# A fused attention kernel: rows of q and k loaded by groups of two pairs, two chunks of values computed after the first scores, no dummy products before them

## What is computed

```
x = x + attn_a(ln(x))    # causal softmax attention, 16 heads of 8, with a position bias
x = x + ffn(ln(x))       # gate r = sigmoid(xr W_r), k = relu(xk W_k)^2, r * (k W_v)
x = x + attn_b(ln(x))    # linear attention: q, k = elu(rope(.)) + 1, kv = sum k v
x = x + ffn(ln(x))

# attn_a, per head h:
attn = q k^T / sqrt(8) + slope[h] * min(key - query, 0)
out  = softmax(attn where key <= query) v ;  out @ W_O.T
```

## Time and profile before

| What | us |
|---|---|
| Median of 3 runs | 347.98 |
| The profiled execution, its own time | 344.1 |
| Its span, first to last instruction | 341.8 |
| Busy: PE, ACT, DVE, POOL | 308.0, 287.1, 164.1, 56.2 |

### The profile page before, as it was taken

The page is one execution under the profiler, slowest core; times in us unless marked ns, Lnnn a source line. Parts: engine busy times, 40 slices in busy tenths (PEclk is TensorE's granted clock), DMA queues, the critical chain, the costliest instruction groups (busy, mean ns, idle before and its releaser), DMA issues.

```text
span 341.8 us, 6101 instructions
## 1 busy us (share of the span) xinstructions
PE 308.0 (90%) x2332; PEld 134.1 (39%) x2332; DVE 164.1 (48%) x426; ACT 287.1 (84%) x409; POOL 56.2 (16%) x56
## 2 busy tenths in 40 slices
PE   3895999999999999999999999999999956889795
PEld 2562232333333223223333223233222836778574
DVE  6851143266634041614340331334530987978785
ACT  7546899998989999999899999989999565882962
POOL 5895000400000000101000100000000161900630
PEclk9997899999999999999999999999999999999999
DMA  7455565850012000000000000000000000000013
GB/s 227 125 148 172 177 189 178 247 163 19 0 44 80 3 0 2 0 2 0 2 4 0 2 0 2 0 2 0 2 1 2 0 3 0 0 2 0 2 32 92
DMA packets 13264, 16.43 MB, mean 48 GB/s; under 512 B 1488, under 2 KB 8016, under 8 KB 13136
## 3 DMA queue, kind: packets, MB, share of 16 engines
q1 hardware_dynamic: 13232, 16.01, 15.5%
HBM read 6.56 MB, written 2.62 MB: 27 GB/s over the span
## 4 chain that ended last, share of the span: by engine, by line
ACT 36%; PE 35%; issue 12%; DVE 7%; SPq 4%; DMA 4%; POOL 1%; ACTq 0%; DVEq 0%
ACT probs L511 23%; PE ps L1062 14%; PE ps L1041 10%; ACT parts_last L511 5%; PE ps L895 5%; ACT x L511 4%; PE ps L890 2%; DMA kr<-parts_mid 2%; PE ps L1119 2%; ACT scr L520 2%; SPq L344 2%; DMA kc<-in_krows 1%; DVE scr L839 1%; SPq L333 1%; POOL rstd L419 1%
## 5 line engine op out<-in xcount | busy, mean ns | idle before, releaser
L511 ACT ACTIVATE probs<-ps 128x1024 f32<-128x1024 f32 (+5 forms) x223 | 169.4, 857 | 13.7 <-PE ps L1041 12.7
L1041 PE MATMUL ps<-qr,kr 64*128 64x512 f32 (+6 forms) x592 | 109.9, 424 | 9.4 <-ACT probs L511 5.2
L1041 PEld LDWEIGHTS ps<-qr,kr 64*128 64x128 f32 x592 | 49.8, 185 | 126.4 <-ACT probs L511 84.5
L1062 PE MATMUL ps<-probs,vaug 128*9 128x512 f32 (+5 forms) x892 | 98.3, 498 | 0.4 <-DVE probs L783 0.4
L783 DVE TENSOR_TENSOR probs<-probs,cs 128x512 f32<-128x512 f32 x60 | 41.2, 689 | 100.1 <-ACT probs L511 100.0
L419 POOL TENSOR_TENSOR rstd<-veps,neghalf 128x4 f32<-128x4 f32 x16 | 16.6, 1036 | 232.7 <-DVE veps L597 232.7
L511 ACT ACTIVATE parts_last<-ps 128x1024 f32<-128x1024 f32 (+9 forms) x49 | 44.9, 971 | 1.4 <-PE ps L1041 1.2
L895 PE MATMUL ps<-w,scr 128*128 128x128 f32 x288 | 35.3, 278 | 3.2 <-ACT scr L470 2.7
L895 PEld LDWEIGHTS ps<-w,scr 128*128 128x128 f32 x288 | 33.5, 192 | 7.0 <-ACT scr L470 3.6
L1062 PE MATMUL ps<-parts_last,vaug 128*9 128x512 f32 (+9 forms) x196 | 25.4, 549 | 0.0
L1062 PEld LDWEIGHTS ps<-probs,vaug 128*9 128x9 f32 x892 | 13.6, 88 | 28.1 <-issue 17.2
(11 more groups left out here) (107 smaller groups left out, 239.0 us busy)
## 6 DMA issues: line engine op xcount, KB each, us to landing
x<-in_x SPq DMA_DIRECT2D x8, 256.0 KB, 4.2
qr<-parts_mid SPq DMA_DIRECT2D x16, 128.0 KB, 3.1
kr<-parts_mid SPq DMA_DIRECT2D x16, 128.0 KB, 3.0
kr<-att SPq DMA_DIRECT2D x8, 128.0 KB, 3.1
qr<-att SPq DMA_DIRECT2D x8, 128.0 KB, 3.2
qr<-parts_last SPq DMA_DIRECT2D x8, 128.0 KB, 3.6
kr<-parts_last SPq DMA_DIRECT2D x8, 128.0 KB, 3.2
out_y<-x SPq DMA_DIRECT2D x4, 256.0 KB, 2.3
```

The costliest lines, as they stand in the source:

```text
L511: nc.scalar.activation(slot[:, 2 * u:2 * u + 2, w0:w1], ps[:, b:b + 2, w0:w1], ACT.Exp).then_inc(exp_done, 1)
L1041: ins = nc.tensor.matmul(ps[:, 2 * (n % 3) + v, w0:w1], kr[kb // TPC][a:a + SIDE, j, P * (kb % TPC):P * (kb % TPC + 1)], qr[unit.c][a:a + ...
L1062: ins = nc.tensor.matmul(ps[32 * v:32 * v + V1, 6 + unit.lane, w0:w1], vaug[:, kb, V1 * h:V1 * (h + 1)], probs_slot(unit)[:, v, w0:w1], st ...
```

## The change

- The product rows are copied by groups of two pairs. A DMA of the same kind carries half the bytes, and there are 16 for each (chunk, q or k), where there were 8. Before the `branched` wait SP issues group 1 of `FIRST` (12 DMAs); behind it groups 2, 3 and 0 of `FIRST` (36 DMAs), then 16 each for the other five tensors. The waits on rows go by group. The heads are permuted in the weights and the mask to suit.
- k of chunk 1 is computed ahead of the turn of chunk 2, and its high part is taken ahead of the copy of that turn. `values(1)` goes to bank 3 and is taken by DVE.
- The values of chunks 2 and 3 are computed behind the branch: chunk 2's between the scores of unit 0 and unit 1, chunk 3's behind unit 1's, both through bank 7 and copied by DVE.
- `branched` no longer waits for all parts, and all 8 dummies of this stretch are gone.
- The slots that the exponentials of units 0, 2 and 3 go to are permuted; ACT waits before unit 3 for the last values.

```diff
-            def product_rows(n, m, side):
+            def product_rows(n, m, g):
...
-                            sp.dma_start(dst[n][PROD_ROW + r:P:STRIDE, PAIRS // 2 * side:PAIRS // 2 * (side + 1), :].bitcast(F32),
-                                         parts[n][m][i][SIDE * side:SIDE * (side + 1), :]).then_inc(rows_loaded[n][m][side], 16)
+                            sp.dma_start(dst[n][PROD_ROW + r:P:STRIDE, 2 * g:2 * (g + 1), :].bitcast(F32),
+                                         parts[n][m][i][P // G * g:P // G * (g + 1), :]).then_inc(rows_loaded[n][m][g], 16)
...
             for n, m in FIRST:
-                product_rows(n, m, 0)
+                product_rows(n, m, ORDER[0][1])
             sp.wait_ge(branched, 1)
-            for n, m in FIRST:
-                product_rows(n, m, 1)
+            for g in (2, 3, 0):
+                for n, m in FIRST:
+                    product_rows(n, m, g)
...
             for n, m in ((0, 0), (2, 0), (2, 1)):
                 constant_rows(n, m)
-                for side in range(2):
-                    product_rows(n, m, side)
+                for g in range(G):
+                    product_rows(n, m, g)
...
+            for n in range(2, NCH):
+                take_values(n, 7)
             for unit in plan:
                 follow(unit)
...
             for n in range(NCH):
                 query_or_key(n, 0)
-                if n:
+                if n == 2:
+                    sum_of_heads()
                     turn_ahead(n)
                 query_or_key(n, 1)
                 if n == 0:
                     fourth_powers()
+                if n < 2:
                     turn_ahead(n)
-                if n == 1:
-                    sum_of_heads()
-                values(n)
-                if n == NCH - 2:
+                    values(n)
+                if n == 2:
...
-            keep_clock(KEEP, 0)
...
-            pe.wait_ge(v_ready[0], NCH // 2)
-            pe.wait_ge(v_ready[1], NCH // 2)
+            pe.wait_ge(v_ready[0], 1)
+            pe.wait_ge(v_ready[1], 1)
+            nc.tensor.matmul(ps[:, 1, 0:2 * P], cb[:, B_ID:B_ID + P], cb[:, 0:2 * P], start=True, stop=True).then_inc(branched, 1)
+            for u in range(2):
+                score(plan[0], u)
             pe.wait_ge(parts_ready, 2 * NCH)
-            nc.tensor.matmul(ps[:, 6, 0:2 * P], cb[:, B_ID:B_ID + P], cb[:, 0:2 * P], start=True, stop=True).then_inc(branched, 1)
-            keep_clock(KEEP, 6)
-            for unit in plan[:2]:
-                for u in range(2):
-                    score(unit, u)
+            values(2)
+            for u in range(2):
+                score(plan[1], u)
+            values(3)
```

More of the change, by code:

```diff
@@ L48 @@
 WARM_UP = 1
-KEEP = 4
 W_Q, W_K, W_V, W_O, W_R, W_KK, W_VV, W_QKV, W_OUT, MU_R, MU_K = (
@@ L382, in _ @@
                 constant_rows(NCH - 1, m)
-                for side in range(2):
-                    product_rows(NCH - 1, m, side)
+                for g in range(G):
+                    product_rows(NCH - 1, m, g)
             sp.wait_ge(flag_ready, 1)
@@ L445, in _ @@
                 for m in range(2):
-                    for side in range(2):
-                        pool.wait_ge(rows_loaded[n][m][side], ROW_LOADS)
+                    for g in range(G):
+                        pool.wait_ge(rows_loaded[n][m][g], ROW_LOADS)
             nc.gpsimd.memset(kr[3].bitcast(F32)[:, :, :], 0.0).then_inc(zeroed, 1)
@@ L500, in exps @@
                 act.wait_ge(pv_done, unit.n + 1)
+                if unit.n == 3:
+                    act.wait_ge(v_psum, NCH)
                 if unit.n == min(other.n for other in plan if other.n % 4 == 1 and not in_x(other)):
                     for m in range(2):
-                        for side in range(2):
-                            act.wait_ge(rows_loaded[NCH - 1][m][side], ROW_LOADS)
+                        for g in range(G):
+                            act.wait_ge(rows_loaded[NCH - 1][m][g], ROW_LOADS)
                 for u, block in enumerate(unit.blocks):
@@ L658, in _ @@
             with dve.If(small == 0):
+                for n in range(2, NCH):
+                    dve.wait_ge(g_values, n - 1)
+                    copy_values(n, n)
                 nc.vector.memset(rden[:, 0:1], 0.0).then_inc(g_max, 2)
@@ L724, in scale @@
                     if k == (place[0, 0], 0)[m]:
-                        for side in range(2):
-                            dve.wait_ge(rows_loaded[0][m][side], ROW_LOADS)
+                        for i in range(G):
+                            dve.wait_ge(rows_loaded[0][m][i], ROW_LOADS)
                 dve.wait_ge(ot_ready, k + 1)
@@ L980, in _ @@
                         pe.wait_ge(const_loaded[n][m], CONST_LOADS)
-                        for side in range(2):
-                            pe.wait_ge(rows_loaded[n][m][side], ROW_LOADS)
+                        for g in range(G):
+                            pe.wait_ge(rows_loaded[n][m][g], ROW_LOADS)
                 for qb in range(TILES):
@@ L1051, in weigh @@
                         pe.wait_ge(ot_ready, 1 + max(ended))
+                    if place[unit.c, unit.g] == 1:
+                        pe.wait_ge(v_ready[0], 2)
+                        pe.wait_ge(v_ready[1], 2)
                     if place[unit.c, unit.g] - 1 in ASIDE:
```

66 lines of the change are left out of this document (35 added, 31 removed).

## The result

The changed kernel takes **364.87 us** in the median of 4 runs (362.91 to 367.08). The kernel before, run beside it on the same chip, takes 348.23 (347.84 to 350.01). The ratio is 1.0587, with a 95% interval of 1.0507 to 1.0668: slower by 16.6 us. The forecast was 361.6, and the time lies 1.9 above the upper end of the range. The direction and the mechanism came as forecast; the wait is longer than the sum made it.

The account below looks back on a forecast made before the run. ACT and PE together were taken to bound the attention loop. Unit 49 12.1 us later plus 1.5 for the clock made +13.6, giving 361.6 us against 347.98; range 345.6 to 363.0.

Parts of the forecast that it names:

- Twice the DMAs on SP: SP's queue after the release: 64 more product issues at 0.63 us each, adding 40.3 us to chunk 3's landing.
- POOL's wait: SP's queue: the wait for POOL's zeroing, 0.8 us beyond 8 issues, would be covered behind 16.
- The restart: ACT behind its wait for chunk 3's rows: PE's clock low again, costing ACT 1.5 us more.
- The values between the first scores: PE at the loop's start: two sets of values, 1.05 us each, partly hidden; cost 0.5, between 0 and 2.1.
- the missing dummies: PE's start: the 8 dummies ran in idle time, 0 for their work; clock effect about 0, between -1.5 and +1.5.
- Rival 1: SP's queue: smaller DMAs issue faster, below 0.51 us each, so no wait and a gain, 346.5 us; chance 0.32.
- the sum for the landing: Chunk 3's last product rows: 77.0 - 2.8 - 0.8 + 40.3 = 113.7 us, when ACT could first write `parts_last`.
- An earlier release: SP's release by PE's `branched` product: at 22.5 instead of 25.29, 2.8 us earlier, bounded by 21.9 and 22.9.
- The landing: Chunk 3's last product rows: they land 3.2 us after the start of their last issue.
- The start: Start of the attention loop: half the bytes before the release bring the first score from 27.98 to 26.0, -2.0 us.
- the forecast's own range: Total time if issues cost near 0.63 us and ACT waits some 12 us: 358 to 363.5 us; chance 0.37.
- SP's last `kr<-parts_mid` issue near 110: Sign in SP's timeline, written there as `kr<-parts_last`: the last such issue would stand near 110 us.

Follow-up runs that it names:

- Experiments 1 to 3: Changed kernel with 84 product issues behind the release, 342.99 us; kernel before with 72 more issues, 369.80 us; changed kernel with 96 issues, 353.82 us.
- The fifth experiment: Changed kernel with PE's `branched` product, which releases SP, moved ahead of PE's branch: 362.33 us, ratio 1.05.
- the last experiment: Changed kernel with 96 waits on an already raised semaphore among PE's first instructions: 366.92 us, one run.

## Why the prediction was wrong

**Right.** "Twice the DMAs on SP" is the large term: the issue went by number and not by bytes (590 ns, and 10.05 for 16 against the forecast 0.63). ACT stands before unit 49, ended by a DMA into `kr`, and unit 49 is late by more than the start gains. Experiments 1 to 3 show it from both sides. POOL's wait is gone. The restart cost 1.6 where 1.5 was taken. The values between the first scores and the missing dummies cost nothing that shows. Rival 1 (cheaper small issues) fell. By the estimate from the Trainium skill, "DMA: Bandwidth & Descriptors", section "Why a DMA increments its semaphore by 16 and not by 1", 0.43 us for an issue, there would be no wait; the trace disagrees, with 590 ns at 64 KB. The same page's "Rules for kernel authors" advise to coalesce small transfers, since under 64 KB one pays mostly overhead. The trace agrees with the advice (halving them all cost 16.6 us), though the price stood in SP's issues, while the DMA share was 0.43 in the wait.

**Wrong: three terms of the sum for the landing.** It gave 113.7; the rows landed at 118.6 and ACT started at 118.8.

1. *An earlier release*, "I take SP's release at 22.5", bounded by 21.9 and 22.9. It came at 24.98: **+2.5**. The step saw that nothing of the work ahead was left, and took the product for free behind it. Before, PE's way over the branch showed as no idle time: the values and the dummies stood there, and the product then waited for DVE. With these gone 1.99 us lie open. The fifth experiment gives the 2.5 back (release 22.49), and unit 49 comes 2.7 earlier with it. The Trainium skill, "Runtime: NRT & Kernel Launch", section "Instruction fetch mechanics", says that a taken branch out of the fetched pages costs a stall for the fetch. Stands of 1.7 to 2.6 us with no releaser in eight of the kernels agree with that, and in each a packet of the instruction queue q8 starts 0.6 to 0.9 us ahead of the stand. What the stand is made of was not separated.
2. *Twice the DMAs on SP*, 64 issues at 0.63, less 0.8: +39.5. From the release to the end of its last issue SP took 49.1 before (25.29 to 74.38) and 92.2 after (24.98 to 117.19): +43.1, so **+3.6**. The price of a quiet issue was right, if a little high (2.44 for four, 10.05 for sixteen). The long issues were missing: the sets of L343 sum to 5.5 above their quiet lengths, in before to 0.75; 4.5 of the 5.5 stand in the five long issues. In before, the packets at 38, 53.5 and 68.5 us fell where SP stood or issued constant rows (one of these took 1.0), and those at 82.5 and 96 behind its queue; a longer queue meets more of them, about one in 15 us. The price to multiply with was 43.9 / 64 = 0.69, with the 0.8 of POOL's wait added back to the 43.1.
3. *The landing*, 3.2 from the start of the last issue: it took 2.04 (116.59 to 118.63), **-1.1**. The 3.2 was a median and not what the last landing took. In the kernel before, the last issue, at 73.77, landed 7.1 later, at 80.88, so that the wait had 20.7 us to spare and not 24.6. There the last of each four landed 4.6 to 10 us behind its issue in 13 of 16 sets, those that SP issues shortly behind constant rows. In the changed kernel the first four `kr<-parts_last` behind the constant rows still took up to 3.7, and the last four about 2. That twelve more issues gave the engines time to work off the constant rows is my reading and not tested. Had the 7.1 stayed, the wait would have been some 5 us longer; that this term came out so near is luck.

The sum, 113.7 + 2.5 + 3.6 - 1.1 = 118.7, is the measured landing within 0.1, and ACT starts 0.2 behind it. With 17.2 + 1.6 = 18.8 in the place of 13.6 the mechanism, and 4.1 for the tail, account for the 22.9 between the spans. The median moved by 16.6 alone: the runs of before beside it lie 3.7 us and more above the profiled one. That this is their tail is likely, and not shown.

**The start** gained more than forecast: -3.0 in the place of -2.0, since the rows were no longer late at all (24.97 lies between the two bounds). All of it went into the wait. At the second place the gain was 2.4 already (56.1 against 58.5): DVE's first `scale` stood 2.5 us for k rows of chunk 0, which the forecast had put at 43.3.

**The range** was too narrow above. Its end, 363.0, leans on a release by 22.9 at the latest, and that bound came from a row in which the branch was covered. The bound that the trace supported was no gain at all, 25.3; with it the forecast's own range would have ended 2.4 higher than 363.5, at 365.9. Two slips changed nothing here: the lower end of that range is 358.9 by its own terms and not 358, and the sign "SP's last `kr<-parts_mid` issue near 110" means `kr<-parts_last` (116.59; the last of `parts_mid` stands at 92.0).

## What to carry to other kernels

Before small DMAs are cut smaller so that the first lands sooner, count the issues on that queue and put the end of the queue beside the last wait on it: on this kernel 84 issues behind the release gain some 1%, 96 lose 2% and 116 lose 6%. For that end, read when the last transfer landed, and not the median of its kind. Cut only those that the start waits for. When work ahead of a branch or a release is taken away, what it covered (here 2 us of PE at the branch) can become the new bound; look for branches and waits that it stood beside.

## What the runs showed of the hardware

- An issue of a strided copy between SBUF tensors into 16 partition rows took SP 589 to 598 ns (medians of `kr<-parts_last`) at 128, 64 and 32 KB.
- Some issues took 0.9 to 1.7 us. In the changed kernel and in the last experiment all 11 from the release on stand within 1 us of a packet of the instruction queue q8, and they moved with the packets. The Trainium skill, "Runtime: NRT & Kernel Launch", section "Instruction fetch mechanics", calls the crossing of a block of instructions mostly hidden. These traces show a price elsewhere: SP's issues beside such a packet were 0.3 to 1.2 us longer.
- PE stood for 1.7 to 2.6 us at a branch over a large body in all eight kernels with the new order, with 4 dummies ahead too (1.97), and for nothing that shows in the three with the old one, where values and dummies stood ahead of it.
- In the kernel before, the last of four product DMAs landed 4.6 to 10 us behind its issue where constant rows stood shortly ahead, and the others about 3. A median per kind hides this.
- The granted clock fell to 0.50 (1.2 GHz) in the tail in some traces only, and for different lengths. The tail took 77.0 us without a fall, 79.9 with 7 us at 0.50 and 81.1 to 81.3 with 10.
